# Attention with ALiBi beside a mixture of experts: wider steps for steep heads, one strided multiply for their diagonals, and sums dealt in runs of 32

## The reference

```
slopes = 2 ** (8 * arange(0, -H, -1) / H)
scores = einsum('bhqd,bhkd->bhqk', q, k) / sqrt(Hd)
probs  = softmax(scores - slopes[:, None, None] * |j - i|)
out    = einsum('bhqk,bhkd->bhqd', probs, v) @ W_out.T + b_out
g      = silu(routed(xn) + shared(xn))      # two of eight experts a token, and the shared one
x      = x + out * g
```

## Time and profile before

| what | us |
|---|---|
| median of 3 runs (1691.61 to 1699.25) | 1693.5 |
| the profiled execution | 1699.23 |
| its span, from the first to the last instruction | 1697.4 |
| TensorE matmuls busy in it | 1532.4 |
| ScalarE busy | 1316.4 |
| VectorE busy | 1012.4 |
| GpSimd busy | 498.6 |

### The profile page before, as it was taken

The page is one execution under the profiler, slowest core; times in us unless marked ns, Lnnn a source line. Parts: engine busy times, 40 slices in busy tenths (PEclk is TensorE's granted clock), DMA queues, the critical chain, the costliest instruction groups (busy, mean ns, idle before and its releaser), DMA issues. The chain is left out here.

```text
span 1697.4 us, 39816 instructions
## 1 busy us (share of the span) xinstructions
PE 1532.4 (90%) x15326; PEld 683.3 (40%) x15328; DVE 1012.4 (60%) x2738; ACT 1316.4 (78%) x1694; POOL 498.6 (29%) x477
## 2 busy tenths in 40 slices
PE   5998998889989999988999999989999999988896
PEld 3555564223334433333444333434443333322364
DVE  7788766988844444445444444454444444568776
ACT  5788777888878888877887878768888888788811
POOL 1222331000023333333443333333333333222143
PEclk9999998999999999999999999989999999999999
DMA  6858775233354454445454444445444454377795
GB/s 204 275 189 262 259 228 156 64 110 89 88 159 139 134 135 134 129 128 133 132 139 121 132 140 135 129 118 139 133 129 129 134 132 132 102 212 216 237 328 175
DMA packets 201087, 265.57 MB, mean 156 GB/s; under 512 B 90960, under 2 KB 158592, under 8 KB 200640
## 3 DMA queue, kind: packets, MB, share of 16 engines
q1 hardware_dynamic: 168256, 171.72, 36.1%
q0 software_dynamic: 24192, 82.86, 15.9%
q10 hardware_dynamic: 8448, 8.39, 1.4%
HBM read 180.56 MB, written 90.46 MB: 160 GB/s over the span
## 5 line engine op out<-in xcount | busy, mean ns | idle before, releaser
L1494 ACT ACTIVATE probs_att<-SC_att 128x1024 f32<-128x1024 f32 (+10 forms) x1306 | 1074.6, 912 | 209.3 <-PE SC_att L1377 179.5
L1403 PE MATMUL O_att<-probs_att,V_att 128*32 128x512 f32 (+7 forms) x8144 | 649.2, 414 | 61.1 <-DVE probs_att L1519 27.2
L1519 DVE TENSOR_TENSOR probs_att<-probs_att,decay 128x128 f32<-128x128 f32 x1024 | 265.7, 287 | 289.5 <-ACT probs_att L1494 246.9
L1403 PEld LDWEIGHTS O_att<-probs_att,V_att 128*32 128x32 f32 x8144 | 180.3, 111 | 221.0 <-issue 145.0
L1334 POOL DMA_INDIRECT ys<-ys_att,back_of_att x144 | 148.2, 1029 | 379.8 <-DVE ys_att L1585 272.1
L1377 PE MATMUL SC_att<-Q,K_turned_att 64*128 64x512 f16 (+7 forms) x1244 | 222.4, 310 | 15.7 <-ACT probs_att L1494 6.8
L1377 PE MATMUL SC_att<-Q,K 64*128 64x512 f16 (+9 forms) x1154 | 201.8, 303 | 10.3 <-DVE K_turned_att L1506 4.9
L1328 POOL DMA_INDIRECT x<-xn,row_of_att x144 | 139.5, 969 | 129.0 <-ACT probs_att L1494 98.2
L1322 POOL DMA_INDIRECT x<-w_rows,owner x72 | 74.0, 1028 | 346.8 <-DVE row_of_att L1568 215.2
L1377 PEld LDWEIGHTS SC_att<-Q,K_turned_att 64*128 64x128 f16 x1244 | 67.4, 94 | 266.3 <-ACT probs_att L1494 159.0
L699 POOL TENSOR_TENSOR inverse<-qk_tok,inverse 128x512 f16<-128x512 f32 x64 | 75.6, 1188 | 169.5 <-ACT inverse L731 162.6
(11 more groups left out here) (210 smaller groups left out, 1672.7 us busy)
## 6 DMA issues: line engine op xcount, KB each, us to landing
K<-k_stack SPq DMA_DIRECT2D x86, 256.0 KB
Q<-q_stack SPq DMA_DIRECT2D x86, 256.0 KB
x<-ys POOLq DMA_DIRECT2D x32, 512.0 KB, 4.8
x<-in_x SPq DMA_DIRECT2D x24, 512.0 KB, 7.2
k_stack<-inverse SPq DMA_DIRECT2D x96, 128.0 KB
q_stack<-inverse SPq DMA_DIRECT2D x96, 128.0 KB
inverse<-k_stack SPq DMA_DIRECT2D x42, 256.0 KB
inverse<-q_stack SPq DMA_DIRECT2D x42, 256.0 KB
```

The lines of the kernel that those rows point to most:

```text
L1403: mm = pe.matmul(O[VW * g:VW * (g + 1), col:col + width * len(mine)], V[par][:, k, :], spans[:, j0:j0 + BPB * (len(mine) - 1) + 1:BPB, :], ...
L1494: nc.scalar.activation(probs[home][:, side + chunk.base:side + chunk.base + chunk.width], SC[:, c % SLOTS, start:start + chunk.width], ACT ...
L1519: v.tensor_tensor(diag, diag, decay[:, head_of(chunk.head), :], ALU.mult).then_inc(faded, 1)
```

## The change

- steps_of joins four key tiles where two neighbours together have at most 512 columns and the next two also have; else two, else one. If a head would have an odd number of steps, the last step of more than one tile is halved. A chunk of four tiles has two in each bank, laid side by side.
- A chunk's diagonals are multiplied by one operation with a strided operand and the table broadcast, where their distances in probs are equal (FADES); else one by one.
- block_of gives 32 in heads 3 to 10 (DEALT); 64 in heads 0 to 2 and 11, 512 in 12 to 15, as before.
- FF_EACH is 11150.

```diff
--- before.py
+++ after.py
@@ -50,7 +50,7 @@
 ROUTE_FROM, SIDE_FROM, NORMS_AT = 8, 8, 5
 PREFIX_TURNS, LIST_TURN, LISTED_AFTER, TILES_AFTER = (31, 36), 61, 136, 16
 FF_APART = (("turn", 2), ("gate", 3), ("down", 4))
-FF_EACH = 11300
+FF_EACH = 11150
 FF_PARTS = {"turn": ("turn", 0), "take": ("turn", 1), "gate": ("gate", 0), "up": ("gate", 0), "tanh": ("gate", 3), "hid": ("gate", 4),
             "down": ("down", 0), "y": ("down", 1)}
 MIX_FROM, MIX_TO = 364, 397
@@ -78,6 +78,7 @@
 FAR = (64, 192, 256, 256, 256, 320, 448, 576, 896, 1216, 1600, 1792)
 LIMITED = len(NEAR)
 LEFT_OUT = 2.0 ** -25
+DEALT = {h: 32 if 3 <= h < 11 else HALF for h in range(LIMITED)}
 ORDER = tuple(x for h in range(H // 2) for x in (h, H - 1 - h))
 STORED = 16 * (BPB + 1)
 
@@ -133,15 +134,17 @@
 
     if head_of(n) >= LIMITED:
         return [(kt,) for kt in range(KT)]
-    small = [window(n, kt)[1] - window(n, kt)[0] <= TB for kt in range(KT)]
+    size = [window(n, kt)[1] - window(n, kt)[0] for kt in range(KT)]
+    fits = lambda kt, count: kt + 2 * count <= KT and max(sum(size[kt:kt + count]), sum(size[kt + count:kt + 2 * count])) <= TB
     steps, kt = [], 0
     while kt < KT:
-        size = 2 if all(small[kt:kt + 2]) and len(small[kt:kt + 2]) == 2 else 1
-        steps.append(tuple(range(kt, kt + size)))
-        kt += size
+        count = 4 if fits(kt, 2) else 2 if fits(kt, 1) else 1
+        steps.append(tuple(range(kt, kt + count)))
+        kt += count
     if len(steps) % 2:
-        last = max(i for i, kts in enumerate(steps) if len(kts) == 2)
-        steps[last:last + 1] = [(kt,) for kt in steps[last]]
+        last = max(i for i, kts in enumerate(steps) if len(kts) > 1)
+        half = len(steps[last]) // 2
+        steps[last:last + 1] = [steps[last][:half], steps[last][half:]]
     return steps
 
 
@@ -204,27 +207,32 @@
         for kts in steps_of(n):
             kt = kts[0]
             if len(kts) > 1:
-                spans = [[(k, *window(n, k)) for k in kts]]
+                half = len(kts) // 2
+                spans = [[[(k, *window(n, k)) for k in side] for side in (kts[:half], kts[half:])]]
             else:
                 lo, hi = window(n, kt)
                 edges = cuts(lo, hi, kt) if limited else range(0, S + 1, TB)
-                spans = [[(kt, *edges[i:i + 2]), (kt, *edges[i + 1:i + 3])] for i in range(0, len(edges) - 1, 2)]
+                spans = [[[(kt, *edges[i:i + 2])], [(kt, *edges[i + 1:i + 3])]] for i in range(0, len(edges) - 1, 2)]
             mine, base = [], 0
-            for (ka, a0, a1), (kb, b0, b1) in spans:
-                runs = [(0, TB - (a1 - a0), ka, a0, a1), (1, 0, kb, b0, b1)]
+            for span in spans:
+                runs, first = [], base
+                for bank, side in enumerate(span):
+                    off = 0 if bank else TB - sum(q1 - q0 for _, q0, q1 in side)
+                    for k, q0, q1 in side:
+                        runs.append((bank, off, k, q0, q1))
+                        at.setdefault((n, k), base)
+                        off += q1 - q0
+                        base += q1 - q0
                 folds = [(bank, off + k * P - q0, k) for bank, off, k, q0, q1 in runs if q0 <= k * P < q1]
-                for bank, off, k, q0, q1 in runs:
-                    at.setdefault((n, k), base + (bank * (a1 - a0)))
                 mine.append(len(chunks))
-                chunks.append(Chunk(n, len(steps), runs, base, a1 - a0 + b1 - b0, folds))
-                base += a1 - a0 + b1 - b0
+                chunks.append(Chunk(n, len(steps), runs, first, base - first, folds))
             steps.append(Step(n, kts, mine))
     return chunks, steps, at
 
 
 def block_of(n):
 
-    return HALF if head_of(n) < LIMITED else TB
+    return DEALT.get(head_of(n), TB)
 
 
 def ring_slots():
@@ -1084,7 +1092,12 @@
 
     CHUNKS, STEPS, AT = plan()
     NC, NS = len(CHUNKS), len(STEPS)
-    FOLDS = [0, *itertools.accumulate(len(c.folds) for c in CHUNKS)]
+    FADES = []
+    for chunk in CHUNKS:
+        at = [AT[chunk.head, k] + k * P - window(chunk.head, k)[0] for _, _, k in chunk.folds]
+        apart = {y - x for x, y in zip(at, at[1:])}
+        FADES.append([(at[0], len(at), apart.pop())] if len(apart) == 1 else [(x, 1, P) for x in at])
+    FOLDS = [0, *itertools.accumulate(len(runs) for runs in FADES)]
     FIRST_CHUNK = [min(i for i, c in enumerate(CHUNKS) if c.head == n) for n in range(BH)] + [NC]
     LAST_STEP = [max(i for i, s in enumerate(STEPS) if s.head == n) for n in range(BH)]
     READ_AT = [None, *(STEPS[CHUNKS[FIRST_CHUNK[n]].step].chunks[-1] for n in range(1, BH))]
@@ -1366,7 +1379,8 @@
                     if c >= SLOTS:
 
                         pe.wait_ge(expd, c + 1 - SLOTS)
-                    todo = [[(off + x0 - q0, k, x0, x1, side) for x0, x1, side in pieces(head_of(n), q0, q1, k)] for _, off, k, q0, q1 in chunk.runs]
+                    todo = [[(off + x0 - q0, k, x0, x1, side) for half, off, k, q0, q1 in chunk.runs if half == bank
+                             for x0, x1, side in pieces(head_of(n), q0, q1, k)] for bank in range(2)]
                     for turn in itertools.zip_longest(*todo):
                         for bank, piece in enumerate(turn):
                             if piece is None:
@@ -1513,10 +1527,16 @@
                     chunk = CHUNKS[c]
                     dve.wait_ge(expd, c + 1)
                     home, side = PLACE[chunk.step]
-                    for _, _, k in chunk.folds:
-                        at = side + AT[chunk.head, k] + k * P - window(chunk.head, k)[0]
-                        diag = probs[home][:, at:at + P]
-                        v.tensor_tensor(diag, diag, decay[:, head_of(chunk.head), :], ALU.mult).then_inc(faded, 1)
+                    table = decay[:, head_of(chunk.head), :]
+                    for at, count, apart in FADES[c]:
+                        if count == 1:
+                            diag = probs[home][:, side + at:side + at + P]
+                            v.tensor_tensor(diag, diag, table, ALU.mult).then_inc(faded, 1)
+                        else:
+                            back = max(0, side + at + count * apart - S)
+                            rows = probs[home][:, side + at - back:side + at - back + count * apart].rearrange("p (n c) -> p n c", c=apart)
+                            diag = rows[:, :, back:back + P]
+                            v.tensor_tensor(diag, diag, table.unsqueeze(1).broadcast_to([P, count, P]), ALU.mult).then_inc(faded, 1)
 
                 def read_out(n):
                     dve.wait_ge(pv, LAST_STEP[n] + 1)
```

## The result

The changed kernel takes 1723.22 us (median of 4 runs, 1714.13 to 1726.82), the one before 1692.55 beside it: a ratio of 1.018, 95% interval 1.0152 to 1.0209. It is slower by 30.7 us, where 5.6 less was forecast. The profiled execution after took 1725.08 us, its span is 1723.3.

What follows compares the result with a forecast made beforehand. TensorE was taken to bound the kernel, with ScalarE next. Batch 0 (-1.5), steep heads (0), runs of 32 (-6.0) and schedule (+1.9) summed to -5.6 us, so 1688 us, own range 1683 to 1692, chance 0.50.

Steps and rivals of the forecast that it cites:

- Diagonals: VectorE's diagonal multiplies: 1024 become 794, four in one 0.61 us instead of 0.80 at pitch; VectorE sheds some 14 us.
- Steep heads: Heads 0 to 2 of batches 1 to 3: K_turned sooner against more sums behind the wait; 0 us, bounds -7 and +5.
- TensorE's account: TensorE at the next head's start: K_turned 0.8 us sooner, 1.0 us more sums left behind the wait; +0.2 us a head.
- Batch 0: Heads 0 to 2 of batch 0: fewer of VectorE's chunk turns before K_turned; -1.5 us, bounds -0.5 and -4.
- Runs of 32: Sums of heads 3 to 10: the fullest column group falls by 5184 columns; -6.0 us, bounds 0 and -8.8.
- weight of 90%: Share counted of the 6.5 us that dealing in 32s saves between 484 and 1500 us, where TensorE leads: 5.8 us.
- Rival 2: At the next head's start: the wait for K_turned decides, with the sums queued behind it; 1693.5 us, chance 0.12.
- Rival 1: Steep heads go by ScalarE's account, its lookahead lasting 2.8 us in place of 1.5; -19.8, 1674 us, chance 0.24.
- Rival 3: Sums of heads 3 to 10: dealing in 32s gives nothing, since groups do not wait for each other; 1694 us, chance 0.06.
- Rival 4: Sums of heads 3 to 10: each run of 32 costs TensorE a step of its own; +19.4, 1713 us, chance 0.08.
- Schedule and stores: Expert tiles move, 12.2 thousand columns go where ScalarE leads: +1.9 us, 0 to +3; store_head's 17,408 more packets: 0, up to +1.

Runs made afterwards that it cites:

- e10: Changed kernel with 15 filling matmuls of 512 columns, results unused, in TensorE's wait for K_turned behind heads of fewer than eight chunks: ratio 1.0104 to the kernel before.
- e4: Changed kernel with K_turned made right behind the first chunk's diagonals, ahead of read_out, in heads of fewer than eight chunks: ratio 0.9951 to the kernel before.
- e1: Kernel before with only the dealing of the sums of heads 3 to 10 in runs of 32 added: ratio 1.0005 to the kernel before.
- e9: Changed kernel with K_turned made right behind the first chunk's diagonals in heads 0 to 5 (fewer than twelve chunks): ratio 0.9933 to the kernel before.
- e8: Kernel before with K_turned made right behind the first chunk's diagonals in heads 0 to 5 (fewer than twelve chunks): ratio 0.9932 to the kernel before.
- e11: Changed kernel where TensorE does the ready sums ahead of the next head's first scores, in heads of fewer than eight chunks: ratio 1.0074 to the kernel before.

## Why the prediction was wrong, by its steps

**Diagonals: right.** The groups of VectorE by shape:

```profile
L1534 DVE TENSOR_TENSOR probs_att<-probs_att,decay 128x128 f32<-128x128 f32 x654 | 182.6, 289 | 291.3 <-ACT probs_att L1508 244.1 <-issue 44.3 <-DVE bounds L1053 0.5
L1539 DVE TENSOR_TENSOR probs_att<-probs_att,decay 128x256 f32<-128x256 f32 x95 | 37.5, 419 | 3.9 <-ACT probs_att L1508 2.7 <-issue 0.8
L1539 DVE TENSOR_TENSOR probs_att<-probs_att,decay 128x512 f32<-128x512 f32 x45 | 30.0, 684 | 9.5 <-ACT probs_att L1508 5.5 <-issue 3.8
```

794 in all; four in one take 684 ns, and two behind each other 1.28 us, the pitch of 0.6 that was taken. Together they take 250.1 us instead of 265.7, 15.6 less where 14 was forecast.

**Steep heads: this step failed.** Forecast 0 for the nine, bounds -7 and +5; measured +30.9 us in the pairs. The steep heads shrank by 8.5 us (7 forecast), but the shallow ones grew by 39.4, not by about as much. Its first half held: in head 0 of batch 3 K_turned came 0.4 us sooner after read_out's start, and over the nine heads it starts 5.7 us after the head's first exponential instead of 6.5, near the 0.8 that was taken. Its second half, TensorE's account, had two faults. It counted only the sums left behind the wait (+1.0 us a head) and set them against VectorE's shorter way. It left out that the sums, the scores of the head's last chunks and part of an expert piece were what TensorE did during that way: 2.81 us of 3.07. In the order of four chunks all of this is either done or stands behind the wait. Over the nine heads the idle time went from 11.0 to 30.5 us, +2.2 a head where +0.2 stood. That the wait would be longer "with 60-odd sum matmuls right behind" stood in the list of what to look for, and it was not priced beyond the queue. The other fault is the clock. It was read from the table by stage (0.95 to 0.98) and called no term. A mean over a stage can't tell that of a stretch with a new idle time in its middle; e10 shows it at some 11 us of the pairs. The sign of the change hung on this step: with the wait gone (e4) the kernel is faster than before.

**Batch 0:** its heads 0 to 2 went from 24.3 to 21.1 us, -3.2 within the bounds of -0.5 to -4, and the three shallow heads behind them grew by 4.8, so more than the gain was lost there. The batch as a whole went from 320.7 to 319.5 us; that this is near the -1.5 of the sum is luck.

**Runs of 32: the price right, the worth not.** A tile of head 8 whose fullest group has 288 columns takes 0.69 us where 320 took 0.73:

```profile
1626.68 0.69 PE L1417 MATMUL O_att<-probs_att,V_att 128*32 128x288 f32 x8
```

The array's work falls by 6.9 to 8.7 us, near the 8.8 that were counted. What failed is the weight of 90%: e1 allows a gain of 3.2 us at most (0.9981), because TensorE's idle time takes up what its work loses. In e1 heads 6 to 10 of batches 1 to 3 have 8.4 us less work and 5.5 us more idle time.

**Rivals.** Rival 2 named the right mechanism, K_turned decides with the sums queued behind it, and gave it 1693.5 us: its bound of +5 was a sixth of what it measured (+30.9), because it too left out the work beside the way and the clock. Rival 1 fell: even with the wait gone (e9), the shallow heads of batches 1 to 3 take back what the steep ones save. Rival 3 is what was measured for the dealing, but not for its reason, since the tiles did get shorter. Rival 4 fell with the 0.69 us. The one mechanism that ended on the slow side was put at the dealing, not at the wait.

**Schedule and stores:** the experts' first matmul comes 6.7 us later after the start of attention (227.1 instead of 220.4), where some 9 were forecast. The stores' packets grew by the 17,408 that were counted, but the queue's share of time went from 36.1% to 36.3%, not up by 3.7 points:

```profile
q1 hardware_dynamic: 185664, 171.72, 36.3%
```

What the schedule and FF_EACH cost in time no run shows by itself; the +1.9 of the sum stays unmeasured.

## What to carry to other kernels

Before a step is joined or a chunk made wider, write down what each engine does between the request for a value and its arrival, not only when it arrives. The same wait cost at most 0.7% with matmuls beside it (e8; 2.81 us of them in the head shown), and without them it cost 2.3% (after 1.018, e4 0.9951). An operation of 0.7 us on which the next head's first work hangs belongs early, here ahead of read_out; that alone gained 0.7% in the kernel before. And an idle time of 3 to 4 us of TensorE is priced with the work at half clock behind it, not by its length alone. Such a price is for one place: four tiles a chunk gained in batch 0 and lost in the others.

## What the runs showed of the hardware

An idle time of TensorE of 3.57 us in the midst of dense work was followed by 10.2 us at half clock; with 15 filling matmuls in the same wait there was none at that head. It does not take one long gap: in e11 three gaps of at most 0.86 us, 2.3 us in all, were followed by it as well, and in one pair of the changed kernel 3.31 us were not. In sums of 64-column matmuls TensorE paused some 0.4 us after every four or five matmuls, four times in a row, with nothing named as its cause. It was so with rounds of 62 and of 31 matmuls.
